# Two attention layers and two expert layers on one core: TensorE's other work moved behind odd heads

## What is computed

```python
x = x + attn_a(layernorm(x))   # causal, 16 heads of 8
x = x + ffn(layernorm(x))      # 8 experts, best 2 per token, hidden 512
x = x + attn_b(layernorm(x))   # not causal, scores shifted and scaled per head
x = x + ffn(layernorm(x))      # the same expert weights

# attn_a, per head
scores = q @ k.T / sqrt(8) + causal_mask
out = softmax(scores) @ v ; out = concat(out) @ wo + bo

# attn_b, per head
q_row_2 = max(sum(|q|, -1)) ** 2 ; k_col_2 = max(sum(|k|, -2)) ** 2
denom = frobenius(q) * max(sum(|x|, -2))
sim = -(q_row_2 - 2 * q @ k.T + k_col_2) / denom
out = softmax(sim) @ v ; out = concat(out) @ W_proj + b_proj
```

## Time and profile before

| | us |
|---|---|
| median of 3 runs | 1134.75 |
| lowest and highest | 1131.26, 1137.76 |
| the profiled execution | 1129.31 |
| its span, first to last instruction | 1127.6 |

### The profile page before, as it was taken

How to read it: one execution, slowest core, us unless ns; L and a number is a source line. 1 busy time by engine, 2 the same in 40 slices (tenths; PEclk the granted TensorE clock), 3 DMA queues, 4 the chain that set the end, 5 groups by cost and what they waited for, 6 DMA issues and landing times.

```text
span 1127.6 us, 28902 instructions
## 1 busy us (share of the span) xinstructions
PE 1002.2 (89%) x9290; PEld 708.7 (63%) x9290; DVE 767.2 (68%) x2334; ACT 676.3 (60%) x1399; POOL 526.9 (47%) x980
## 2 busy tenths in 40 slices
PE   2999999997989999999798888998989799999990
PEld 1455555453568999999443444444444689999990
DVE  4788888968776333456778998999867663334443
ACT  2377777663644555556287878998948445555550
POOL 3244444433733700454676765556817346005565
PEclk9999999987989999999688989999968899999995
DMA  5454657442146977987643433433311469778974
GB/s 153 112 123 123 160 132 175 130 108 64 47 151 185 288 229 233 275 256 222 145 99 84 108 87 100 84 92 88 97 20 54 152 205 282 220 236 268 275 229 116
DMA packets 201723, 175.03 MB, mean 155 GB/s; under 512 B 19812, under 2 KB 160616, under 8 KB 201576
## 3 DMA queue, kind: packets, MB, share of 16 engines
q1 hardware_dynamic: 193384, 156.41, 50.0%
q0 software_dynamic: 8192, 16.79, 4.9%
HBM read 122.99 MB, written 50.14 MB: 154 GB/s over the span
## 4 chain that ended last, share of the span: by engine, by line
PE 62%; DVE 16%; issue 7%; DMA 5%; SPq 5%; POOL 4%; ACT 1%; POOLq 0%; DVEq 0%; ACTq 0%
PE psS L1378 9%; PE psT L1385 9%; PE psS L355 8%; PE psO L321 7%; DVE mx L671 5%; PE psO L1401 4%; PE psN L1401 4%; PE psS L386 4%; PE psT L363 2%; PE psM L276 2%; PE psN L328 2%; POOL xn L1279 2%; PE psM L426 2%; DMA xin<-xg 2%; POOL xg L1265 1%
## 5 line engine op out<-in xcount | busy, mean ns | idle before, releaser
L671 DVE TENSOR_REDUCE mx<-psS 128x3 f32<-128x384 f32 (+1 forms) x512 | 310.4, 617 | 78.3 <-PE psS L386 45.6
L355 PE MATMUL psS<-kst,qst 48*128 48x256 bf16 (+1 forms) x1024 | 196.7, 280 | 42.5 <-DVE mx L671 30.2
L558 ACT ACTIVATE pT<-psT,scb 128x512 f32<-128x512 f32 x256 | 194.0, 773 | 51.7 <-PE psT L363 48.8
L1442 DVE TENSOR_TENSOR hT<-sg,psT 128x512 f32<-128x512 f32 x142 | 97.4, 686 | 152.1 <-PE psT L1385 123.7
L363 PE MATMUL psT<-qst,kst 50*128 50x256 bf16 (+1 forms) x1024 | 192.4, 273 | 4.4 <-DMA qst<-scr_m 2.3
L1265 POOL DMA_INDIRECT xg<-xn,slot x128 | 123.5, 965 | 130.9 <-DVE ysb L1437 69.6
L1378 PE MATMUL psS<-xTt,wgc 128*128 128x128 f32 x1136 | 153.1, 278 | 4.7 <-issue 4.7
L553 ACT ACTIVATE pT<-psT 128x384 f32<-128x384 f32 x256 | 123.2, 488 | 54.2 <-PE psT L363 46.2
L355 PEld LDWEIGHTS psS<-kst,qst 48*128 48x128 bf16 x1024 | 62.6, 96 | 143.0 <-DVE mx L671 77.6
L1385 PE MATMUL psT<-xTt,wuc 128*128 128x128 f32 x1136 | 151.5, 277 | 0.0
L790 POOL TENSOR_SCALAR_AFFINE_SELECT pT<-pT 128x256 f32<-128x256 f32 x224 | 91.4, 415 | 116.8 <-ACT pT L553 116.1
(11 more groups left out here) (225 smaller groups left out, 1599.2 us busy)
## 6 DMA issues: line engine op xcount, KB each, us to landing
wgc<-in_L_ffn_Wg SPq DMA_DIRECT2D x142, 256.0 KB
wuc<-in_L_ffn_Wu SPq DMA_DIRECT2D x142, 256.0 KB
scr_part<-part SPq DMA_DIRECT2D x128, 128.0 KB, 2.4
qst<-scr_part SPq DMA_DIRECT2D x64, 192.0 KB, 3.7
kst<-scr_part SPq DMA_DIRECT2D x64, 192.0 KB, 4.6
xin<-xg SPq DMA_DIRECT2D x142, 64.0 KB
eo<-ysb SPq DMA_DIRECT2D x142, 64.0 KB
scr_part<-part SPq DMA_DIRECT2D x32, 192.0 KB, 2.4
```

The lines of the kernel that those rows point to most:

```text
L355: return nc.tensor.matmul(ps[:, c0:c0 + n], q_[r64, t, q0], k_[r64, t, 0:n], start=(half == 0), stop=True, skip_group_check=True)
L558: nc.scalar.activation(pT[:, g % 8, 0:cols], psT[g % 2][:, 0:cols], ACT.Exp, scale=scb[r][:, 0, i:i + 1], bias=scb[r][:, 1, i:i + 1]).then ...
L671: nc.vector.tensor_reduce(mx3[:, u, 0:n, pos:pos + 1].rearrange("p a b -> p (a b)"), psS[h % 2][:, 0:kcols(L)].rearrange("p (a k) -> p a k ...
L1442: nc.vector.tensor_tensor(out=hT[(n0 + k) % FETCH][:].rearrange("p a c -> p (a c)"), in0=sg[p][:], in1=psT[p][:], op=ALU.mult).then_inc(f[ ...
```

## The change

Only places in the loop over heads change; every piece keeps its instructions and its waits. PV quads 0 and 1 go from behind heads 6 and 10 to behind 7 and 11. In the first layer the transposes of x go from head 2 to 3. The v projection goes from 12 to 13. In the second layer the sum over q goes from 14 to 15, directly ahead of the transposes of row sums. The first half of the output goes from heads 4, 6 and 8 to 3, 5 and 7, and the second half's projection from 14 to 15. Within one head the order is that of the code: at head 3 the transposes of x and then the output transposes, at 5 the q and k projections and then the transpose of the normalised output, at 7 PV and then the projection, at 11 PV and then the output transposes, at 13 PV, v and the transpose, at 15 the sum over q, the row sums and the projection.

```diff
@@ -388,7 +388,7 @@
                                               start=False, stop=True, skip_group_check=True)
                 if S_:
                     last_s.then_inc(s["S"], 1)
-                if T_ and h in (6, 10, 13):
+                if T_ and h in (7, 11, 13):
                     pv_quad(bT, rT, (h - 5) // 4)
                 if h == 1:
                     if T_:
@@ -409,11 +409,11 @@
                                                 prow[0:1, 2, 8 * u:8 * u + 8], ones_row[0:1, 0:1],
                                                 start=False, stop=True, skip_group_check=True)
                     last.then_inc(s["bc_ps"], 1)
-                if h == (2 if L.causal else 3) and P_:
+                if h == 3 and P_:
                     pe_xT(pe, L, j)
                 if h == 5 and P_:
                     pe_qk(pe, L, j)
-                if h == 12 and V_:
+                if h == 13 and V_:
                     if not L.causal:
                         after(pe, s["bc"], 2 * (j - 1))
                     after(pe, s["m2"], 2 * bS + 1)
@@ -426,20 +426,20 @@
                         last = nc.tensor.matmul(psM[:, k * P:(k + 1) * P], xT[rS][:, k * P:(k + 1) * P],
                                                 L.w_in[:, 2, :], start=(k == 0), stop=True, skip_group_check=True)
                     last.then_inc(s["v_ps"], 1)
-                if h == 14 and P_ and not L.causal:
+                if h == 15 and P_ and not L.causal:
                     pe_qsum(pe, L, j)
                 if h == 15 and P_ and not L.causal:
                     pe_rows(pe, L, j)
-                if h == 4 and O_:
+                if h == 3 and O_:
                     after(pe, s["oT"], 2 * bO + 2)
                     if T_:
                         after(pe, s["m2"], 2 * (bT + 1))
                     else:
                         after(pe, s["x1"], 2 * bO)
                     out_transposes(0)
-                if h == 6 and O_:
+                if h == 5 and O_:
                     out_transpose_on(0)
-                if h == 8 and O_:
+                if h == 7 and O_:
                     out_project(0)
                 if h == 9 and S_:
                     after(pe, s["mxu"] if L.causal else s["mx"], 2 * bS + 1 if L.causal else 16 * bS + 8)
@@ -453,7 +453,7 @@
                     out_transposes(1)
                 if h == 13 and O_:
                     out_transpose_on(1)
-                if h == 14 and O_:
+                if h == 15 and O_:
                     out_project(1)
                 if L.pe_hook:
                     L.pe_hook(pe, j, h)
```

## The result

| | before | after |
|---|---|---|
| median, us | 1133.40 (4 runs) | 1187.32 (4 runs) |
| lowest and highest | 1131.26, 1137.76 | 1182.12, 1190.48 |
| ratio, with its 95% interval | | 1.045 [1.042, 1.049] |
| the profiled execution | 1129.31 | 1182.12 |
| TensorE busy, share of the span | 1002.2, 89% | 1019.8, 86% |

The account below looks back on a forecast made before the run. Second-layer steps were held bound by TensorE, VectorE and ScalarE within 1 us, first-layer steps by TensorE alone. Waits summed to 37 us, giving 1166 or 1172; forecast 1171, own range 1150 to 1183, over all 1140 to 1196.

Parts of the forecast that it names:

- first layer, steps with all pieces: First attention layer, 12 steps: waits for the output transposes and the normalised output, +0.7 us a step, 8.4 in all.
- second layer, steps 2 and 3: Second attention layer: the row-sum wait alone in two steps at the ends, 1.1 us.
- second layer, steps 4 to 15: Second layer, 12 steps: 8 clean ones at 2.2 us, 17.6, and four with long VectorE combinations at 1.5, 6.
- The walk through the step: Second layer, from head 14 to the next step's head 8: each moved piece's waits followed, +2.2 us a clean step.
- All four waits: TensorE idle in a second-layer step: row transposes 0.6 us, output transposes 0.55 late, normalised output's transpose 0.65, projection 0.4.
- the row sums' wait: Line 293 behind head 15: row transposes wait for VectorE's maximum over the q-sum, idle 0.6 us, next head 0 +0.55.
- What is left ... keeps the same ScalarE work and I leave it: Second layer, from head 8 to the next head 14, 6.4 us: left unpriced, no cost added.
- The ends: Both layers' ends: two steps each without new q and k, nothing hiding the normalised output's wait, about 1 each, 4 us.
- Rival 3: Second layer: with TensorE idle more often, granted clock falls to 1.2 GHz in 6 of 12 steps, +21 us, 1192; chance 0.12.
- rival 1: New waits over before TensorE asks, so the saving counts: 0.63 us in some 14 steps, 9 us, 1126; chance 0.11.
- the saving: Second layer: changes of tiling fall from 31 to 24 a step, 7 x 0.09 = 0.63 us; nothing saved in the first layer.

Follow-up runs that it names:

- u_sums: The changed kernel with the sum over q and the second half's projection put back behind head 14; 1177.4 us, ratio 1.036 to the kernel before.
- u_both: The changed kernel with the first half of the output, the sum over q and the second projection all put back; 1147.8 us, ratio 1.013 to before.
- m_v: The kernel before with only the v projection moved from behind head 12 to 13; 1141.8 us, ratio 1.005.
- u_out: The changed kernel with the first half of the output put back behind heads 4, 6 and 8; 1160.2 us, ratio 1.023 to the kernel before.
- only_A: The kernel before with the change made in the first attention layer alone; 1156.3 us, ratio 1.019.
- f_rows: The changed kernel with the second projection ahead of the row sums' transposes behind head 15; 1173.8 us, ratio 1.032 to the kernel before.
- m_pv0x: The kernel before with only the first PV quad moved from head 6 to 7 and the first layer's x transposes from 2 to 3; 1143.0 us, ratio 1.006.
- f_eng: The changed kernel with VectorE's low maxima and normalisation and ScalarE's copy of the transposed output also one head earlier; 1148.5 us, ratio 1.012 to before.
- late_odd: The kernel before with the second layer's output pieces and PV later, at odd heads, sum over q and v one head earlier; 1160.2 us, ratio 1.022.

## Why the prediction was right, and where its terms were off

Forecast and measurement from profile to profile, 1129.31 to 1182.12 (steps from first scores to first scores):

| term | forecast | measured |
|---|---|---|
| first layer, steps with all pieces | 8.4 (12 x 0.7) | 9.2 in steps 4 to 14 |
| end of the first layer, from step 15 to the last transposed scores | 2 | 4.1 |
| second layer, steps 2 and 3 | 1.1 | 0.8 |
| second layer, steps 4 to 15 | 23.6 | 28.7, of it 7 in steps 14 and 15 at the lower clock |
| end of the second layer, from step 16 to the last transposed scores | 2 | 3.7 |
| the rest: the start, and from the last transposed scores of each layer on (the expert layers above all) | 0 | 6.3, of it 5.2 behind the transposed scores |
| sum | 37 | 52.8 |

The steps are numbered as in the code; the prediction counts the same 12 as 5 to 16. Before the change, six of these in the second layer took 16.7 to 17.2 us and six 18.0 to 24.4, not eight and four as the prediction has it; at its own prices that is 1.4 us less.

**The walk through the step held.** All four waits stand where the code's order put them, each 0.0 to 0.2 us from its forecast. The clean step grew by 2.03 (16.75 to 18.78) where I had 2.2, though one part is made up differently: the row sums' wait is 0.61 as forecast, but u_sums shows that it adds some 0.3 to the step, not 0.55.

**"What is left ... keeps the same ScalarE work and I leave it" failed.** The 6.4 us behind head 8 hold v and the second PV quad. In u_both, which keeps these, a clean step is 0.54 longer than before; m_v shows that the move of v alone adds 0.6, as VectorE's addition didn't move. The clean step's sum came out near the truth by luck: this term, missing, and the row sums and the first half, too dear (0.29 and 1.27 as u_sums and u_out give them back, against 0.55 and 1.65), set each other off. The same walk, carried on to head 13 and asking not only what a moved piece waits for but who waits for it, would have given it.

**The ends were mis-sized.** I gave them 4 us in both layers together; in the changed kernel they took 7.8 more. To its last transposed scores the first layer's end took 4.1 us more there, 9 to 12 more in the profiled executions of u_sums, only_A and f_rows, which have the first half's new places there too, and 0.4 to 4.0 more in the nine kernels that keep or restore at least part of it. Steps without q and k have nothing to hide lines 328 and 333 behind, as I wrote, but I priced two steps with a guess instead of reading them in the trace. What follows the transposed scores keeps its order but for one projection, and its 5.2 us are not explained by a moved piece: the stretch up to the second layer took 0.1 to 5.2 us more than in the profile of before in all 13 other kernels, and that profile lies 6 us under the median of its kernel.

**The clock was a rival and turned out to be a part.** Rival 3 had the mechanism and the place (long steps of the second layer): steps 14 and 15 took 24.58 and 22.00 at 0.83 and 0.73, against 21.06 and 18.51 in u_sums, 7 us. The 1187 measured lies nearer to its 1192 than to my 1171. How much of the whole is the clock's can be estimated: within the runs of one kernel, over all 14 kernels, a mean granted clock lower by 0.01 goes with some 6 us. After's four runs have a mean of 0.918, the last 22 of before one of 0.932: some 9 us of the 51 between their means. This is a correlation: no run changed the clock alone, and a longer wait may be what lowers it. With 9 us taken off, 42 are left, beside the 37 forecast. TensorE's busy time, 17.6 us longer for as many matmuls, says that the clock's part may be larger; how much of it lengthened the execution is not shown.

**The rivals that fell.** The waits were not hidden (rival 1): they stand in the trace at nearly their forecast lengths. And the saving shows nowhere: no kernel with fewer changes of tiling has a clean step under the 16.69 of before. None of them is free of new waits, so what a change of tiling is worth by itself stays open; m_pv0x has one change more in a step of the second layer, and waits for nothing new there, and its clean step is the 16.69 of before. The Trainium skill, TensorEngine Tiling (Array Packing), section PSUM Bottleneck, says that packing the array speeds up TensorE and leaves the emptying of PSUM as it is. The runs agree as far as they go: one of the 512 maxima, with which VectorE empties the banks of scores, took 617 ns before and 618 after. The forecast of 1171 lay 16 us low of 1187, inside its range and beyond the forecast's own 1183: the direction and the mechanism were right, the ends were too small, and v and the clock were missing.

## What to carry to other kernels

Where engines work in order and meet at semaphores, a piece that moves in one engine's list takes its partners with it or waits for them: list for each moved piece what it waits for and who waits for it, and move those too: in f_eng, which did, 39 of 52 us came back, some of them with the clock. Time freed on one engine can be worth no more than the slack of the next one, here 0.62 us of VectorE in a step, and work gathered behind one head must be shorter than what the consumer has in stock, here two banks of scores. Price the first and last steps of a pipeline from their own rows; they had less cover here than the ones between. And look in the trace of a counter-test for the waits that it was built to avoid: late_odd had 25 us of new ones.

## What the hardware showed that I had not expected

The granted clock of TensorE differs from run to run of the same program, and several us go with it: the runs of before go from 1131.0 us at a mean of 0.936 to 1142.4 at 0.923. The same code in the same place can fall or not: the first layer's end has the same order in after and in only_A, and its mean clock was 0.88 in the one and 0.78 in the other. So a difference of 5 us between two profiles of this kernel says little by itself; in m_pv0x clean steps are those of before and the median is 6 us higher.
